# A three-stage Perceiver kernel: six quarters of the context loaded turned, tile 0's readout ahead of a quarter of tile 1, and four VectorE steps of the attention in another order

## What is computed

```
x = x + xattn(layernorm(x), ctx, mask)      # x: 32 x 32 x 1024, ctx: 32 x 257 x 1024
x = x + attn(layernorm(x), Wq, Wk, Wv, Wo)  # 16 heads of 64, causal over 32 tokens
x = x + ffn(layernorm(x), w_gate, w_up, w_down)   # hidden width 4096, silu(gate) * up

def xattn(q, ctx, mask):
    scores = einsum('bsd,bmd->bsm', q, ctx) / sqrt(D)
    scores = where(mask[:, None, :], scores, -1e30)
    return einsum('bsm,bmd->bsd', softmax(scores), ctx)   # 0 where no mask entry is set
```

## Time and profile before

| | us |
|---|---|
| median of 3 runs | 1507.94 |
| lowest, highest | 1506.26, 1508.06 |
| the profiled execution | 1506.29 |
| its span | 1504.5 |
| TensorE busy | 1477.5 (98%) |
| VectorE, ScalarE, GpSimd busy | 766.9, 555.1, 869.7 |

### The profile page before, as it was taken

The page is one execution under the profiler, slowest core; times in us unless marked ns, Lnnn a source line. Parts: engine busy times, 40 slices in busy tenths (PEclk is TensorE's granted clock), DMA queues, the critical chain, the costliest instruction groups (busy, mean ns, idle before and its releaser), DMA issues.

```text
span 1504.5 us, 23233 instructions
## 1 busy us (share of the span) xinstructions
PE 1477.5 (98%) x7988; PEld 1203.7 (80%) x7988; DVE 766.9 (51%) x1232; ACT 555.1 (37%) x1099; POOL 869.7 (58%) x712
## 2 busy tenths in 40 slices
PE   7999999999999999999999999999999999999998
PEld 5766887887878888888888888888888888888886
DVE  5776054162261496935626626526536436436446
ACT  4557132132231254334344343343433343433442
POOL 1233211302212121389789788788798798798795
PEclk9999999999999999999999999999999999999999
DMA  9992200101201000021111111111121121121123
GB/s 380 400 367 97 83 29 28 56 28 38 74 0 56 29 1 22 20 65 56 49 63 56 49 63 49 56 63 49 51 67 49 42 77 38 53 70 35 56 63 112
DMA packets 42950, 114.18 MB, mean 76 GB/s; under 512 B 4896, under 2 KB 5152, under 8 KB 40480
## 3 DMA queue, kind: packets, MB, share of 16 engines
q1 hardware_dynamic: 42480, 113.27, 22.1%
q10 hardware_dynamic: 432, 0.39, 0.1%
HBM read 109.45 MB, written 4.19 MB: 76 GB/s over the span
## 4 chain that ended last, share of the span: by engine, by line
PE 95%; DVE 2%; DMA 1%; issue 1%; SPq 1%; ACT 0%; DVEq 0%
PE ps L1281 38%; PE ps L1301 18%; PE ps L940 10%; PE ps L941 9%; PE ps L942 9%; PE ps L974 3%; PE ps L1014 2%; PE ps L992 2%; PE ps L1082 1%; DMA ctx<-in_ctx 1%; PE ps L946 1%; PE ps L1125 1%; DVE x L1702 1%; SPq L344 0%; DVE x L1478 0%
## 5 line engine op out<-in xcount | busy, mean ns | idle before, releaser
L557 POOL TENSOR_TENSOR b_lo<-blk,b_hi 128x512 fp32r<-128x512 f32 x180 | 231.8, 1295 | 49.8 <-ACT b_hi L835 41.2
L1702 DVE TENSOR_TENSOR x<-ps,x 128x1024 f32<-128x1024 f32 x210 | 242.2, 1211 | 0.0
L470 POOL TENSOR_TENSOR w_lo<-raw,w_hi 128x2048 fp32r<-128x2048 f32 x16 | 73.3, 4584 | 287.5 <-ACT w_hi L677 287.5
L1281 PE MATMUL ps<-xT_hi,b_hi 128*128 128x512 f32 x480 | 186.7, 389 | 0.0
L1281 PE MATMUL ps<-xT_lo,b_hi 128*128 128x512 f32 x480 | 186.7, 389 | 0.0
L1281 PE MATMUL ps<-xT_hi,b_lo 128*128 128x512 f32 x480 | 186.7, 389 | 0.0
L1301 PE MATMUL ps<-b_hi,b_hi 128*128 128x512 f32 x420 | 166.5, 396 | 0.0
L1301 PE MATMUL ps<-b_lo,b_hi 128*128 128x512 f32 x420 | 163.8, 390 | 0.0
L1301 PE MATMUL ps<-b_hi,b_lo 128*128 128x512 f32 x420 | 163.6, 389 | 0.0
L1676 DVE TENSOR_TENSOR hid<-ps,kept 128x512 f32<-128x512 f32 x60 | 41.5, 692 | 233.7 <-PE ps L1281 193.8
L557 POOL TENSOR_TENSOR b_lo<-s_sum,b_hi 128x512 fp32r<-128x512 f32 x105 | 136.2, 1297 | 35.9 <-ACT b_hi L835 35.9
(11 more groups left out here) (155 smaller groups left out, 3227.6 us busy)
## 6 DMA issues: line engine op xcount, KB each, us to landing
blk<-in_blocks SPq DMA_DIRECT2D x180, 256.0 KB, 2.7
ctx<-in_ctx SPq DMA_DIRECT2D x64, 512.0 KB, 10.1
raw<-in_w SPq DMA_DIRECT2D x19, 1024.0 KB, 4.8
x<-in_x SPq DMA_DIRECT2D x8, 512.0 KB, 7.2
ext_row<-in_ext SPq DMA_DIRECT2D x8, 512.0 KB, 13.2
out<-x SPq DMA_DIRECT2D x16, 256.0 KB, 2.6
mask<-in_mask ACTq DMA_DIRECT2D x1, 224.9 KB, 6.0
extT<-in_ext_t ACTq DMA_DIRECT2D x1, 128.0 KB, 4.4
```

Source lines behind the costliest of these rows:

```text
L470: pool.tensor_tensor(w_lo[wslot][:, :], raw[slot][:, :], w_hi[wslot][:, :].bitcast(F32), ALU.subtract).then_inc(split_done[slot], 1)
L557: pool.tensor_tensor(b_lo[slot][:, :], src[:, :], b_hi[slot][:, :].bitcast(F32), ALU.subtract).then_inc(block_lo, 1)
L1281: mm = pe.matmul(ps[:, bank, :], stat[a], moving[b], start=first and m == 0, stop=(s == 3 and m == 2), skip_group_check=True)
L1702: dve.tensor_tensor(part, ps[:, bank:bank + 2, :], part, ALU.add).then_inc(down_added, 1)
```

## The change

Six quarters of the context, the first of tiles 4 to 7 and the second of tiles 6 and 7, are no longer turned by TensorE. The host lays them out turned, with the column of row 257 in its place, and SyncE loads each with one transfer of 1032 KB straight into its `cT` buffer (8256 bytes for each partition). For these quarters the transposes, the evictions and GpSimd's column copy are gone, and the scores wait for the transfer. The transfer waits until the scores that last used the buffer are done. It stands in SyncE's program between the two halves of the next tile's context; tile 7's two stand behind the sixth extra row. The first weight pair now comes behind tile 7's context.

TensorE's `readout(0)` now precedes quarter (1, 2). In the attention VectorE's `heads_lo` stands ahead of the mask at steps 2 and 3 in all groups, and in groups 0 to 2 `add_projected` of tile 4 stands ahead of the mask at step 7.

```diff
@@ constants
+LOADED = ((4, 0), (5, 0), (6, 0), (6, 1), (7, 0), (7, 1))
...
@@ -255,11 +258,18 @@
         def by_act(c):
             return 2 if c % KP == 2 else 3
 
+        def by_pe(c):
+            return (c // KP, c % KP) not in LOADED
+
+
+        def turned_before(c):
+            return sum(by_pe(i) for i in range(c))
+
         def act_before(c):
-            return c // KP * 11 + (0, 3, 6, 8)[c % KP]
+            return sum(by_act(i) for i in range(c) if by_pe(i))
 
         def dve_before(c):
-            return c * BT - act_before(c)
+            return turned_before(c) * BT - act_before(c)
 
 
         ROW_BANKS = (6, 6, 0, 2, 6, 2, 6, 2)
...
@@ -348,6 +358,14 @@
                 for h in range(2):
                     for b in range(BT):
                         context(t, h, b).then_inc(ctx_full[t % RING][h], 16)
+
+            def loaded(t):
+                for j in range(KP):
+                    if (t, j) in LOADED:
+                        c = t * KP + j
+                        sync.wait_ge(scores_done, c - RING + 1)
+                        n = LOADED.index((t, j))
+                        sync.dma_start(cT[c % RING][:, :, :, :], turned_in[n]).then_inc(turned_full[n], 16)
 
             def extra_rows(t):
                 sync.dma_start(ext_row[t % 2][:, :], ext_in[t]).then_inc(ext_full[t % 2], 16)
...
@@ -362,12 +380,18 @@
             tile(2)
             extra_rows(1)
             for t in range(RING, NT):
+                sync.wait_ge(readout_done, t - RING + 1)
+                sync.dma_start(x[:, t, :], x_in[:, t, :]).then_inc(x_full[t % 4], 16)
+                for b in range(BT):
+                    context(t, 0, b).then_inc(ctx_full[t % RING][0], 16)
+                loaded(t - 1)
+                for b in range(BT):
+                    context(t, 1, b).then_inc(ctx_full[t % RING][1], 16)
                 if t == NT - 1:
                     sync.dma_start(raw[0][:, :], w_in[0]).then_inc(raw_full[0], 16)
-                sync.wait_ge(readout_done, t - RING + 1)
-                tile(t)
                 sync.wait_ge(ext_added, t - RING + 1)
                 extra_rows(t - 1)
+            loaded(NT - 1)
             sync.wait_ge(ext_added, NT - 2)
             extra_rows(NT - 1)
             sync.wait_ge(scores_done, NT * KP)
...
@@ -472,9 +496,11 @@
 
             def ext_columns(t, j):
                 c = t * KP + j
+                if not by_pe(c):
+                    return
                 if c == 0:
                     pool.wait_ge(ext_t_full, 16)
-                pool.wait_ge(c_psum, c * BT + 1)
+                pool.wait_ge(c_psum, turned_before(c) * BT + 1)
                 pool.tensor_copy(cT[c % RING][:, :, :, MB],
                                  extT[:, 2 * j:2 * j + 2, t * BT:(t + 1) * BT].rearrange("p e b -> p b e"))\
                     .then_inc(ext_column, 1)
...
@@ -636,8 +662,10 @@
 
             def context(t, j):
                 c = t * KP + j
+                if not by_pe(c):
+                    return
                 for b in range(by_act(c)):
-                    act.wait_ge(c_psum, c * BT + b + 1)
+                    act.wait_ge(c_psum, turned_before(c) * BT + b + 1)
                     act.activation(cT[c % RING][:, b, :, 0:MB], ps[:, b, :].rearrange("p (e m) -> p e m", e=2), ACT.Copy)\
                         .then_inc(c_act_done, 1)
 
...
@@ -960,14 +988,17 @@
 
                 if t and j % 2 == 0:
                     pe.wait_ge(ctx_full[t % RING][j // 2], (t // RING + (t % RING > 0)) * BT * 16)
+                if not by_pe(c):
+                    return
+                before = max((i for i in range(c) if by_pe(i)), default=None)
                 for b in range(BT):
                     if t == 0 and j % 2 == 0:
                         pe.wait_ge(first_full[j // 2][b], 16)
-                    if c:
-                        if b < by_act(c - 1):
-                            pe.wait_ge(c_act_done, act_before(c - 1) + b + 1)
+                    if before is not None:
+                        if b < by_act(before):
+                            pe.wait_ge(c_act_done, act_before(before) + b + 1)
                         else:
-                            pe.wait_ge(c_dve_done, dve_before(c - 1) + b - by_act(c - 1) + 1)
+                            pe.wait_ge(c_dve_done, dve_before(before) + b - by_act(before) + 1)
                     for e in range(2):
                         at = (2 * j + e) % 4 * P
                         for m in range(MT):
...
@@ -977,9 +1008,12 @@
 
             def scores_of(t, j):
                 c = t * KP + j
-                pe.wait_ge(c_act_done, act_before(c + 1))
-                pe.wait_ge(c_dve_done, dve_before(c + 1))
-                pe.wait_ge(ext_column, c + 1)
+                if by_pe(c):
+                    pe.wait_ge(c_act_done, act_before(c + 1))
+                    pe.wait_ge(c_dve_done, dve_before(c + 1))
+                    pe.wait_ge(ext_column, turned_before(c + 1))
+                else:
+                    pe.wait_ge(turned_full[LOADED.index((t, j))], 16)
                 if j == 0:
                     pe.wait_ge(next_act_done, t + 1)
                     pe.wait_ge(next_dve_done, t + 1)
...
@@ -1041,8 +1075,11 @@
                 context(t + 1, 0)
                 context(t + 1, 1)
                 probabilities(t)
-                context(t + 1, 2)
+                if t:
+                    context(t + 1, 2)
                 readout(t)
+                if t == 0:
+                    context(1, 2)
                 scores_of(t + 1, 0)
                 scores_of(t + 1, 1)
                 context(t + 1, 3)
...
@@ -1347,8 +1384,10 @@
 
             def context(t, j):
                 c = t * KP + j
+                if not by_pe(c):
+                    return
                 for b in range(by_act(c), BT):
-                    dve.wait_ge(c_psum, c * BT + b + 1)
+                    dve.wait_ge(c_psum, turned_before(c) * BT + b + 1)
                     dve.tensor_copy(cT[c % RING][:, b, :, 0:MB], ps[:, b, :].rearrange("p (e m) -> p e m", e=2))\
                         .then_inc(c_dve_done, 1)
 
...
@@ -1521,17 +1560,19 @@
 
                 if not last:
                     for st in range(NT - 1):
+                        if 2 <= st <= 3:
+                            heads_lo(WITH_SCORES[st])
                         mask_scores(st)
-                        if st >= 2:
+                        if st > 3:
                             heads_lo(WITH_SCORES[st])
                         if st >= 3:
                             add_projected(g, st - 3)
                         turn_probabilities(st)
                         if st == 3:
                             heads_lo(2)
+                    add_projected(g, NT - 4)
                     mask_scores(NT - 1)
                     heads_lo(NT - 2)
-                    add_projected(g, NT - 4)
                     turn_probabilities(NT - 1)
                     add_projected(g, NT - 3)
                     heads_lo(NT - 1)
...
@@ -1541,9 +1582,11 @@
                 for st in range(NT + 2):
                     if st == NT - 1:
                         turned_lo(2, st - 4)
+                    if 2 <= st <= 3:
+                        heads_lo(WITH_SCORES[st])
                     if st < NT:
                         mask_scores(st)
-                    if 2 <= st < NT:
+                    if 3 < st < NT:
                         heads_lo(WITH_SCORES[st])
                     if st >= 4 and st != NT - 1:
                         turned_lo(2, st - 4)
```

More of the change, by code:

```diff
@@ L44, with build @@
 FIRST_ADDS, ADDS = 2 * NT, 14
-def build(nc, x_in, ctx_in, w_in, block_in, mask_in, ext_in, ext_t_in, out):
+LOADED = ((4, 0), (5, 0), (6, 0), (6, 1), (7, 0), (7, 1))
+def build(nc, x_in, ctx_in, w_in, block_in, mask_in, ext_in, ext_t_in, turned_in, out):
     stack = ExitStack()
@@ L180, in build @@
         next_dve_done = sem("next_dve_done")
+        turned_full = [sem(f"turned_full{i}") for i in range(len(LOADED))]
         c_psum = sem("c_psum")
@@ L1757, with turned @@
         .reshape(NT * 2 * BT, P, MT, HALF)
+    def turned(t, j):
+        part = ctx[t * BT:(t + 1) * BT, :, j * 2 * P:(j + 1) * 2 * P].reshape(BT, M, 2, P).transpose(3, 0, 2, 1)
+        return np.pad(part, ((0, 0), (0, 0), (0, 0), (0, MB + 2 - M)))
     def tiles_of(w, first, n):
@@ L1801 @@
         "ext_t": np.ascontiguousarray(ctx[:, MB].T.reshape(KD, P, B).transpose(1, 0, 2)),
+        "turned": np.ascontiguousarray(np.stack([turned(t, j) for t, j in LOADED])),
     }
```

## The result

| | before | after |
|---|---|---|
| median of 6 runs each, us | 1507.10 | 1499.22 |
| lowest, highest | 1506.15, 1508.06 | 1497.53, 1501.64 |
| profiled execution | 1506.29 | 1498.38 |
| its span | 1504.5 | 1496.6 |

What follows compares the result with a forecast made beforehand. TensorE was taken to bound the attention; its transposes and the transfers, nearly equally, the context's stage. Attention's -13.0 us and the context's +0.6 gave -12.4, so 1495.5 us against a median of 1507.94; 8-in-10 range 1491.5 to 1502.

Steps and rivals of the forecast that it cites:

- Tile 4's addition: Attention, groups 0 to 2, step 7: adding tile 4's projection ahead of the last mask shortens TensorE's wait, 7.6 us gained.
- The clock in the attention: Attention: half-speed stretches behind the 2.77 us wait in the second and third groups go with it, 3.3 us gained.
- The heads: Attention, step 2: the heads' low parts ahead of the mask remove four TensorE waits of 0.46, 1.8 us gained.
- the loss of 0.2 a group at step 3: Attention, groups 0 to 2: mask 3 queues behind a wait for tile 1's heads, delaying project(1); 0.5 us lost in all.
- The last group: Attention's last group, step 3: TensorE's wait for heads that come late goes, 0.8 us gained there.
- The swap: Context, tile 0: readout ahead of tile 1's third quarter delays the last scores 3.2 us; half clock loses 1.5 more.
- The transfers' price: Context: each turned quarter of 1032 KB takes 2.6 us of the queue at 408 GB/s; bounds 2.5 and 4.2.
- the second rival: Context: transfers with 8256-byte rows take 3.0 to 3.6 us each, 3 to 5 us longer, 1498 to 1501; chance 0.17.
- the fourth: Context, tiles 6 and 7: turned transfers at half rate or worse, 5.2 us each, kernel slower at 1510; chance 0.04.
- The chain of landings: Context, tiles 4 to 7: queued transfers' landing times against TensorE's needs; (5,0) just in time, waits of 1.9 and 1.7 at tile 6.
- -0.9 as forecast: Context's stage: six loads and tile 0's earlier readout together, before any clock loss, shorten it by 0.9 us.
- the first: Context, tile 0: wait or clock drop absent, so loads bring up to 3 to 4 us, 1491 to 1494; chance 0.22.

## Why the prediction was half right

- **Tile 4's addition, 7.6 us: right.** 0.24 of the wait remained against 0.23 expected, in each of three groups, and GpSimd's margin was 0.18 against 0.2.
- **The clock in the attention, 3.3: right as a size, less certain than it was put.** Groups 1 and 2 shortened by 4.6 and 4.7 us, group 0 by 3.1; the 1.6 between them is the half clock. The kernel with the swap alone, and the one with the heads alone, show that one to three groups may pay it, so that two was the count of one trace.
- **The heads: right, with a smaller by-effect.** Of the 3.06 us in group 0, 2.53 are the addition's and 0.46 the heads', and 0.07 are left over: the loss of 0.2 a group at step 3 isn't there. The last group was mis-sized: it was to win 1.26 and won 0.62. The 0.8 us wait at step 3 is gone, and TensorE waits 0.72 for normalised rows from ScalarE instead, just ahead of that place:

```profile
522.29 1.09 PE L974 MATMUL ps<-ident,xn 128*128 128x128 f32 x8 [0.72 <-ACT xn L760]
```

- **The swap, 3.2 + 1.5: right, and the largest thing that the change has against it.** The idle stretch was 3.79 us, the last scores started at 41.88 against 41.8 expected, and tile 2's first quarter at 45.33 in place of 40.53, 4.80 later. Swapped alone it cost 4.6 us of the stage.
- **The transfers' price, 2.6 us: right.** 2.51 was measured, so the second rival (3.0 to 3.6) is out, and the fourth too. By the rule of the Trainium skill ("DMA: Bandwidth & Descriptors", section "Anatomy of one DMA"), 2.0 us and the bytes at 436 GB/s, it would be 4.4 each, an estimate. The 2.51 don't agree with that rule taken for each transfer of a full queue: the fixed part isn't paid one after another here. The waits for probabilities behind two loaded quarters, put at 1.4, were 1.27 and 1.26.
- **The chain of landings: the step that failed.** It had (5, 0) land at 96.0, "just in time"; it released TensorE only at 99.37, after a wait of 1.52. Two things are missing. The 1.5 us of half clock in tile 0 were added to the sum at its end, but not to the release that lets SyncE issue tile 5's x: that came 4.80 us later, not 3.2, which makes 1.6. And the chain ran at 408 GB/s behind its first landing, while the queue moved 251 from 73 to 76, which is 1.2 us, with 0.5 more in smaller parts. Why it was slow there is open. That it had run dry isn't enough: before, and with tile 0's wait filled, it had run as dry and was back within 3 us. With three loaded and the swap, x is issued at 70.05 and the queue is slow in the same stretch (269 from 73 to 76). The fill shows the first part: with it both the 1.6 and the slow stretch went, and so did the wait at tile 5. The two parts are 3.3 us together, which reach tile 6: its second quarter's scores start at 117.12, 3.1 us later than the 114.0 forecast.
- **The second half clock: not in the prediction.** Two waits at tile 6 were forecast, 1.9 and 1.7 us, but priced by their length alone; they were 1.48 and 1.43, with only 1.07 of work between them. 3.08 us of work at half speed cost 1.5 us. The stage then follows from the transfers: -0.9 as forecast, 3.1 for the later landings (the half clock of tile 0 is inside them, and so was wrongly added by itself), and 1.5 here make +3.7; +3.8 was measured. That this trace fits so well is in part luck, since half clocks come and go between executions.
- **The feed-forward, 1.3 us: not foreseen**, and its cause is open.

Of the rivals, the first (no wait or no clock drop in tile 0) was refuted by the rows. The kernel without the swap shows what it would have been: six loads then do shorten the stage by 3.6 us in the profiled executions, as that rival has it, but the medians with them (1493.64) and without (1493.36) don't differ. 1.3 us go in the feed-forward, and the mean clocks (0.997 in two of four runs) say that most of the rest goes in half clocks. The forecast gave the loads 10.5 us of transposes and kept 4.1; the median kept none of it until the second quarters were left out, and then, with four loaded, 4.2.

The fastest kernels here are those with three or four first quarters loaded, no swap, and the attention's new order: 1488.2 to 1489.2 us, 10 to 11 us below the changed kernel.

## What to carry to other kernels

A delay in a stage of two near-equal bounds must be carried through both chains, with all its parts: what TensorE loses to the clock also delays the release that the transfer queue waits for. Move work off the busiest engine only as far as nothing else becomes the limit: where the softmax between two of its steps sets the pace, a saved transpose turns into a wait. Consider several short waits close together as one idle stretch, and expect the clock's part to come and go from one execution and one kernel to the next.

## What the runs showed of the hardware

- The granted clock fell to 1.2 GHz behind 2.77 us of idle TensorE in one, two or three of three like places, by kernel. It fell also behind two waits of 1.48 and 1.43 us with 1.07 us of work between them, in the changed kernel, and not behind the same two waits (1.72 and 1.44) in the profiled execution without the swap. Waits of 0.59 and 1.27 us at tile 7 took it in one kernel and not in another.
- 32 transposes of the identity in a wait of 3.8 us kept the granted clock at 1.00.
- Transfers of 1032 KB standing one behind the other in a full queue landed 2.51 us apart.
- A queue that had run down to 66 GB/s was back at 412 GB/s 3 us after the next transfer's issue in one place, and at 400 only after 6 us in another, with 251 GB/s for 3 us in between; why is open.
- The loop of the feed-forward, with the same instructions and no wait in the profile, took 843.4 to 843.5 us in place of 842.0 to 842.4 with six quarters loaded some 500 us earlier.
